# Moving the preparation of the second token group behind the first softmax rounds of a sliding-window attention stage

## The reference, cut to what matters

```python
NHEAD, HEAD_DIM, WINDOW = 16, 16, 128
q = (x @ Wq.T)...; k = (x @ Wk.T)...; v = (x @ Wv.T)...
# each chunk of 128 queries attends to its own and the previous chunk of 128 keys
scores = jnp.einsum('bhcid,bhcjd->bhcij', qc, k2) / jnp.sqrt(D)
scores = jnp.where(valid, scores, -jnp.inf)      # band of 128 keys
attn = jax.nn.softmax(scores, axis=-1)
out = jnp.einsum('bhcij,bhcjd->bhcid', attn, v2)
x = _layernorm(x + out @ Wo.T)
```

## Time and profile before

| what | value |
|---|---|
| median of 3 runs | 2736.73 us (2736.68 to 2738.42) |
| the profiled execution: its time / its span | 2736.73 us / 2734.7 us |
| TensorE busy, whole program | 2430.2 us (89%) |
| VectorE / ScalarE / GpSimd busy | 1984.8 / 1497.0 / 1311.3 us |
| mean granted TensorE clock | 0.949 |
| sliding-window stage | from 1621.3 to about 2037 us |
| opening loop (rounds 0 to 6) of that stage | 1621.4 to 1642.8 us |
| score wait of TensorE for the maxima in 1664 to 1954 us | 13.3 us in 24 waits |
| wait of `back` for the normalised mix, same stretch | 9.4 us in 12 waits |

### The profile page before, as it was taken

The page is one execution under the profiler, slowest core; times in us unless marked ns, Lnnn a source line. Parts: engine busy times, 40 slices in busy tenths (PEclk is TensorE's granted clock), DMA queues, the critical chain, the costliest instruction groups (busy, mean ns, idle before and its releaser), DMA issues. The chain is left out here.

```text
span 2734.7 us, 43890 instructions
## 1 busy us (share of the span) xinstructions
PE 2430.2 (89%) x14525; PEld 1449.1 (53%) x14525; DVE 1984.8 (73%) x4362; ACT 1497.0 (55%) x3321; POOL 1311.3 (48%) x1257
## 2 busy tenths in 40 slices
PE   4668989898989898979999988899868999999897
PEld 1224444444444443557777755656644665566555
DVE  3999999999999999636767647777764444455545
ACT  5666777777777775433333324444545556654522
POOL 1777777777777777423333323444563222221411
PEclk7899999999999999989999988999988999999999
DMA  5343333333433334210000034243212000000100
GB/s 160 124 130 120 133 122 126 122 126 121 126 120 125 121 128 132 62 46 28 1 1 1 13 74 81 51 71 68 53 34 71 19 17 17 17 17 17 48 14 9
DMA packets 134306, 195.93 MB, mean 72 GB/s; under 512 B 23953, under 2 KB 58898, under 8 KB 134082
## 3 DMA queue, kind: packets, MB, share of 16 engines
q1 hardware_dynamic: 132098, 190.24, 24.2%
q0 software_dynamic: 960, 2.62, 0.3%
q10 hardware_dynamic: 1024, 0.26, 0.1%
HBM read 153.95 MB, written 13.63 MB: 61 GB/s over the span
## 5 line engine op out<-in xcount | busy, mean ns | idle before, releaser
L398 POOL TENSOR_TENSOR ma_seen<-ma_state,ma_cs 128x1024 f32<-128x1024 f32 x256 | 603.3, 2360 | 330.6 <-DVE ma_state L951 312.2
L951 DVE TENSOR_TENSOR_SCAN ma_state<-ma_decay,ma_last,ma_drive 128x512 f32<-128x512 f32 x512 | 650.4, 1271 | 1.3 <-ACT ma_decay L803 1.2
L587 PE MATMUL ma_acc<-ma_seen,ident 128*128 128x512 f32 x1024 | 487.7, 606 | 49.5 <-POOL ma_seen L398 49.3
L938 DVE TENSOR_TENSOR ma_drive<-ma_weight,ma_bs 128x512 f32<-128x512 f32 x512 | 356.8, 697 | 45.0 <-ACT ma_weight L793 16.6
L587 PEld LDWEIGHTS ma_acc<-ma_seen,ident 128*128 128x128 f32 x1024 | 194.4, 195 | 301.6 <-issue 212.7
L803 ACT ACTIVATE ma_decay<-ma_dt,ma_a_neg 128x512 f32<-128x512 f32 x512 | 338.0, 708 | 0.1
L2076 DVE CUSTOM_DVE_ANT_0 sw_score<-sw_score,both_band 128x256 f32<-128x256 f32 (+1 forms) x512 | 197.7, 449 | 50.2 <-PE sw_score L1890 39.0
L2014 ACT ACTIVATE sw_prob<-sw_turned 128x512 f32<-128x512 f32 (+1 forms) x256 | 135.5, 581 | 171.9 <-PE sw_turned L1904 147.6
L104 POOL TENSOR_TENSOR moe_h_low<-both_V,light_wqkv 128x512 fp32r<-128x512 f32 x80 | 105.1, 1313 | 247.3 <-DVE light_wqkv L100 239.9
L1812 POOL TENSOR_SCALAR_AFFINE_SELECT sw_prob<-sw_prob 128x512 f32<-128x512 f32 x128 | 84.7, 661 | 206.5 <-ACT sw_prob L2014 206.5
L1536 DVE TENSOR_TENSOR both_V<-both_V,moe_up 128x512 f32<-128x512 f32 x80 | 55.0, 687 | 120.5 <-PE moe_up L1325 79.4
(11 more groups left out here) (547 smaller groups left out, 5474.7 us busy)
## 6 DMA issues: line engine op xcount, KB each, us to landing
ma_bs<-bc_rows SPq DMA_DIRECT2D x256, 256.0 KB, 3.2
ma_cs<-bc_rows SPq DMA_DIRECT2D x256, 256.0 KB, 3.2
both_wide<-both_kh SPq DMA_DIRECT2D x28, 192.0 KB, 4.4
both_wide<-both_qh SPq DMA_DIRECT2D x20, 256.0 KB, 4.5
x_rows<-X SPq DMA_DIRECT2D x1, 4096.0 KB
light_rows<-li_y SPq DMA_DIRECT2D x32, 128.0 KB, 1.7
out_dram<-li_o SPq DMA_DIRECT2D x32, 128.0 KB, 1.8
X<-in_L_attn_x_dram SPq DMA_DIRECT2D x1, 3584.0 KB, 14.5
```

Source lines behind the costliest of these rows:

```text
L398: g.tensor_tensor(out=seen[n % RR][:, :, :], in0=state[n % SR][:, :, :], in1=each(cs[n % CR][:, :], 2), op=ALU.mult).then_inc(S["seen_full ...
L587: ins = t.matmul(accs(mm), K["ident"][:, :], seen[n % RR][:, mm, :], start=False, stop=(n % NS == NS - 1))
L938: v.tensor_tensor(out=drive[mm][:, :], in0=weight[mm][:, :], in1=bs[n % CR][:, :], op=ALU.mult).then_inc(S["drive_done"], 1)
L951: v.tensor_tensor_scan(state[n % SR][:, mm, :], decay[s % DR][:, :], drive[mm][:, :], last[:, k, m:m + 1], ALU.mult, ALU.add).then_inc(S[" ...
```

## The change

It empties the opening loop of preparation: `slide_lead` is gone. In its place group 1 is prepared in steps 0 and 1 of the main loop, and in q and k steps the second half moves from round 2 to round 1. The `turn` of step 0 stands after opening round 3, as before, and the opening rounds 4 to 6 follow it. The engines' loops follow the same order.

```diff
     order = []
-    for R in range(LEAD):
-        order += [(kind, 1, m) for kind, m in slide_lead(R)]
-        if R == ROUNDS - 1:
-            order.append(("turn", 0, 0))
+    order.append(("turn", 0, 0))
...
-def slide_lead(R):
-    return {0: (("xT", 0), ("xT", 1)), 1: (("q", 0),), 2: (("q", 1),), 3: (("k", 0),), 4: (("k", 1),),
-            5: (("v", 0), ("v", 1)), 6: (("v", 2),)}[R]
-
 def slide_ahead(n):
     if n == 0:
-        return ((0, "v", 1, 3),)
+        return ((0, "xT", 1, 0), (0, "xT", 1, 1), (1, "q", 1, 0), (1, "q", 1, 1), (2, "k", 1, 0), (3, "k", 1, 1))
     if n == 1:
-        return ((3, "xT", 2, 0), (3, "xT", 2, 1))
+        return ((0, "v", 1, 0), (1, "v", 1, 1), (2, "v", 1, 2), (3, "v", 1, 3),
+                (3, "xT", 2, 0), (3, "xT", 2, 1))
     j, a = (n + 7) // 4, (n + 7) % 4
...
     if a == 1:
-        return ((0, "q", j, 0), (2, "q", j, 1), (3, "v", j, 0))
+        return ((0, "q", j, 0), (1, "q", j, 1), (3, "v", j, 0))
     if a == 2:
-        return ((0, "k", j, 0), (2, "k", j, 1), (3, "v", j, 1))
+        return ((0, "k", j, 0), (1, "k", j, 1), (3, "v", j, 1))
...
-            for R in range(LEAD):
+            for R in range(ROUNDS):
                 scores(R)
-                for kind, m in slide_lead(R):
-                    ahead(kind, 1, m)
-                if R == ROUNDS - 1:
-                    turn(0)
+            turn(0)
+            for R in range(ROUNDS, LEAD):
+                scores(R)
```

More of the change, by code:

```diff
@@ L2026, in finish @@
                 a_.activation(xc(n), y[n % 2][:, :], ACT.Identity, scale=rstd[:, :], bias=offset[:, :]).then_inc(S["x_done"], 1)
[L2028 to L2035, removed]
+            shift(0)
             for n in range(STEPS + 2):
@@ L2128, in _ @@
                 maxes(R)
[L2129 to L2133, removed]
             for n in range(STEPS + 2):
```

## The result

| | runs | lowest | median | highest |
|---|---|---|---|---|
| before, same chip | 4 | 2736.68 | 2737.57 us | 2740.28 |
| changed | 4 | 2772.83 | 2777.95 us | 2789.83 |

The ratio is 1.0141, interval 1.0104 to 1.0179: slower, as forecast, but by 40 us where 16 were. The profiled execution of the changed kernel took 2759.47 us (span 2757.4), 22.7 more than that of before, so one program gives times 30 us apart. Both facts have to be explained. The result lists 21 executions of the changed kernel, the profiled one and the four of the table among them. The profiled one is the fastest: five lie at 2759.5 to 2764.3 us with a mean granted clock of 0.944 to 0.951, sixteen at 2769.3 to 2789.8 with 0.930 to 0.945, the four with 0.930 to 0.940. The one execution of 3694 us in the table of the experiments ran at a mean clock of 0.605 and is left out of the ratios.

A forecast was written before the change was run, and what follows sets the result against it. The prediction took TensorE's order of work, with its gaps and clock, to bound the sliding stage. To 2736.73 us it added +7.1 (opening), +7.7 (second halves) and +1.5 (clock behind the stall), +16.3, giving 2753 us, 80% range 2741 to 2764.

The forecast's parts named there:

- Bare rounds: Opening: seven rounds without preparation, four of 1.93 us and three of 2.53, gaining 5.8 us at first.
- q halves ready: Group 1's q halves, now prepared in the main loop, ready at about 1649.0, against 1633.25 when SyncE issued before.
- Rival (c): The placing hides: group 1's pairs land quickly and only the steps cost, 2745 us; chance 9%.
- six dependent pairs: Group 1's placing on SyncE's queue: a chain taking 26.8 us, ending at 1675.8, so `scores(16)` waits some 6 us.
- 1644.88: Time in the profile before until which the forecast had group 1's q pairs run, from 1633.25.
- The bank list: q steps: q1 takes front's bank and waits for the mix, `turn` waits for q1's split; round 3's scores +0.56 us.
- Rival (a): q and k steps: the moved half covers the waits, 21 us back against +7, 2723 us; chance 4%.
- The small transfers: q and k steps: two small transfers may meet q_places' large ones and land late; upper bound 1.1 us per step.
- My 7.7: Second halves in round 1: +0.7 us per step, +7.7 us over the other eleven steps, bounds 4.4 to 12.
- another 0.4: q step: round 3's `shifted` waits for ScalarE's late exponentials until 11.07 instead of starting at 10.74.
- The work behind the stall: After the `scores(16)` wait: +1.5 us for halved clock, bounds 0 and 7; step 2's other waits about -0.3.
- Clock in those steps: q and k steps: idle time more in sum but less dense; nothing entered, bounds -12 and +8 us.

The follow-up runs named there:

- turn_first: Kernel before, with second halves in round 1 but behind `turn` in TensorE's order and bank list, split behind round 2's maxima; median 2736.4 us, ratio 1.0000.
- after_third: The changed kernel run again, unaltered, for another profile; median 2779.6 us, ratio 1.0110 against the kernel before.
- after_again: The changed kernel run once more, unaltered, for a second profile; median 2760.7 us, ratio 1.0105 against the kernel before.
- halves_only: Kernel before with only the second halves moved to round 1, opening as before; median 2756.0 us, ratio 1.0061.
- halves_hold: Kernel before with second halves in round 1, and SyncE holding groups 2 to 7's q placing until the next step's first shifted scores; median 2764.9 us, ratio 1.0061.
- lead_only: Kernel before with only the bare opening loop, second halves staying in round 2; median 2749.1 us, ratio 1.0034.
- lead_unchained: Bare opening with second halves in round 2, SyncE issuing all pairs of a group's placing at once, a semaphore each; median 2749.7 us, ratio 1.0046 against before.

## Why the prediction was off

Right, by its own steps:

- Bare rounds 1.89 and 2.53 us (forecast 1.93 and 2.53), round 7's scores after 15.5 us (15.6).
- q halves ready 26.5 us after the first scores (27.6), the placing 28.8 us long (26.8), a wait of 6.4 us before `scores(16)` (about 6), which comes 8.1 us later (7.4). Rival (c) falls, and with it the estimate by the Trainium skill's formula for a transfer (DMA: Bandwidth & Descriptors, section "Anatomy of one DMA — SWDGE (gpsimd) path"): the six pairs took 28.8 us, not 16. That fit is for transfers that GpSimd issues, and these are SyncE's. But "six dependent pairs" was right in its length and not in its reason: the first k pair does not wait for the third q pair, and issued all at once the pairs still take 25.7 us. For the same reason 1644.88 is no landing of the q pairs, as I read it, but the issue of the first k pair.
- The bank list: q1 waits 0.72 for the mix (0.8), `turn` 1.38 for the split (1.3), at 7.70 us after q0 (7.78), round 3's scores at 10.37 (10.40). Rival (a) falls; turn_first shows that with the half behind `turn` these two waits go and the 0.93 us before round 2's scores are covered, but the 0.8 before `back` stays, and new waits for VectorE and ScalarE leave 0.05 us of the 1.75 in step 10. It moves TensorE's order, the bank list and the split together, so which of them decides is not shown apart.

Mis-sized, within the waits:

- The small transfers. I wrote that they might meet the large ones and land too late, as a bound, and entered nothing. They did: 1.3 us in step 10, and 3.0 us of waits in the profiled execution's three. With them the waits of steps 3 to 23 cost 8.6 us at before's clock, where I had 7.7. My 7.7 is also a little high by its own figures: the "another 0.4" is 11.07 - 10.74 = 0.33, which gives 0.62 a step and 6.8 in all.
- The work behind the stall: 3.7 us more to step 3 (8.1 to 11.85), where I had -0.3 and +1.5 (and the 1.2 and 0.5 that I named make 1.7). The window shows the clock, and the q half there takes 3.45 us for 1.98:

```profile
1670.00:1678.00 8.00, 6.16 (x34) 3.53 (x34) 2.05 (x9) 1.83 (x4) 1.22 (x2) 0.57 0.23 42
```

Added up for the profiled execution: 11.85 to step 3 (I had 8.6), 8.6 of waits in steps 3 to 23 (7.7) and 6.4 of clock in them (0) make the stage's 26.9 us, where I had 16.3. The stage before it was 5.0 shorter and the one behind 0.8 longer in this execution, which gives the 22.7. That the profiled time, 2759.5, lies within 7 us of my 2753 owes something to those 5.0 us.

The step that failed is "Clock in those steps", where I wrote "I enter nothing". I priced the clock only where the order changed, at what a low stretch costs there. Even there it came to +6.4 us in the profiled execution and to about nothing in after_third. The steps behind it, 25 to 31, have no projections, are untouched by the diff, and stand in no part of the prediction; there the clock can stay low for six steps, costs 4.4 us a step and came to 23.6 in after_third. The profiled execution has nothing of it and was 7 us over my forecast; the median is 18 higher still. That low clock makes this difference is shown by the clocks of the runs (0.930 to 0.940 for 0.951). That it lies in the last steps of the four timed runs is inferred from after_third, whose profiled execution has a time and a clock like theirs (2781.7, 0.934). By times and clocks, with no profile of each run, one of four in after_again had it and most of after_third. Of before's 119 runs beside the experiments 24 lie above 2750 us, from none of 26 on one chip to twelve of 29 on another.

Open: why the changed kernel falls into that stretch so much more often. Halves_only and halves_hold are in it in their profiles and lead_only in part of it, turn_first for one step. More idle time in the q and k steps goes with it in halves_only and halves_hold, but lead_only's are before's there (27.7 us idle for 27.4) and it falls too, and from step 25 until the clock falls the waits are the same in all of them (0.85, 0.28 and 0.25 us a step), and no run separates the idle time from the moment at which the stage reaches its last steps. That it differs between chips or moments (before's own median lay between 2737.6 and 2744.9) is seen, not explained.

## What to carry to other kernels

Before moving work between two points, write down who takes the shared buffers in which order: a unit moved ahead of another hands it its own wait. When a producer of a transfer is moved later, count back from the consumer all the transfers that must land before it, ask whether their order or their bytes set the time, and which small transfers will now be issued beside large ones. And read several executions, and compare the profiled one's time with the median: here it was the fastest of 21. A region that the diff doesn't touch can be where the clock decides.

## What the runs showed of the hardware

- The clock can stay low under full work. In after_third TensorE was busy 99% of 56 us and the granted clock stayed at 0.50 in all of it. The work there is 48- and 49-row scores, 128x32 mixes and a few transposes. The Trainium skill (TensorE: Matmul & The Clock Gate, section "What's actually happening") says that activity releases the throttle; in these 56 us it did not, though TensorE was busy. With one or two 128x512 matmuls added to each of these steps, none of seven profiles shows the stretch in them; without, five of eleven show it in part or in whole.
- Two 4 KB transfers issued on ScalarE's queue while SyncE's 256 KB pairs are in flight came late enough to hold TensorE for 1.16 us, and for 4.87 us once all pairs were issued at once.
- In 1656 to 1666 us DMA moved 104 GB/s where each of SyncE's pairs waited for the one before (lead_only), and 125 GB/s where they were issued at once (lead_unchained), though DMA's busy share rose from 0.65 to 1.11.
